# One list of 689 steps replaced by another list of the same steps, in a transformer layer with test-time training

## The chip, the core and the metric

The kernel runs on one core of a Trainium2 chip. Its time is the device time of that core in microseconds, the median of three executions. The profile is one further execution, taken by the hardware profiler.

## The reference

Four sequences of 512 tokens, width 256, all float32. One layer is attention plus feed-forward, each with layer norms and a residual:

```
x = x + layernorm(attn(layernorm(x)))
x = x + layernorm(ffn(layernorm(x)))        # ffn: gelu(x @ proj1.T + b1) @ proj2.T + b2, hidden width 1024
```

`attn` adds two parts and multiplies the sum by `Wo`. One is a sliding-window softmax attention (window 128, two heads of 128). The other carries, for every sequence and each of four heads, three 64x64 weight matrices through the sequence in chunks of 128 tokens. After each chunk its gradient is orthogonalised by five Newton-Schulz passes and the weights are updated:

```
for a, b, c in NS_COEFFS:                   # five times
    A = X @ X.T
    B = b * A + c * (A @ A)
    X = a * X + B @ X
W = renorm(W + X)                           # row norms kept
```

So chunk c+1's small products wait for chunk c's passes; the rest of the layer does not depend on them.

## The kernel before

Everything is cut into 4 chunks of 128 tokens, and each chunk into steps. A step is named by a kind, its chunk and one or two numbers: `NB.2.0.1` is kind NB in chunk 2, pass 0, matrix group 1. One list, `ORDER` (line 137), holds all steps of all chunks. Each engine walks the same list from front to back and issues its own part of every step (the `run(ORDER)` at the end of each engine's block). Parts are tied by semaphores. So the list sets the order on all five queues at once: an engine that waits in one step holds whatever it has behind it. Which PSUM bank a step writes is also worked out from the list (`bank_plan`), the one free longest first, and the step waits for that bank's last reader.

The kinds that matter here, with the line of TensorE's product and the engine that reads it:

- `TX` (L682): transposes X for all heads, four products 128x128; ScalarE copies it to XT (L816).
- `NA` (L691): X times its transpose, 16 products of 64x64 tiles, four at a time in the quarters of the array; VectorE makes A of it (L1056).
- `NB` (L701): A times A, 16 of them; VectorE makes B (L1056).
- `NX` (L713): B times X, 16 of them; ScalarE scales it back into X (L959), in the last pass VectorE adds the weights.
- `RN`, `RM`, `WX` (L723): row norms (a power on GpSimd), scaling on VectorE, transposes of the new weights. Three matrix groups (the last number) go through each of these on their own.
- `FW` (L629), `GB` (L604), `DH` (L617), `OUT` (L643), `DW` (L662): the other small products of a chunk; `MU`, `MR`, `SS` (L673), `SN`: the gradient's norm and X's first value.
- `XT`, `QK` (L559), `VV` (L568), `TR` (L591), `S` (L732), `PT` (L739), `PV` (L748), `CT` (L755), `WO` (L763), `NT` (L770): projections and window attention, with whole 128x128 tiles.
- `F1` (L782): one eighth of the first feed-forward product, GELU on ScalarE (L1034); `F2` (L793): the second, for one sequence; `F2N`: its norm and residual, then a store.

ScalarE keeps one function table at a time and loads another where a step asks for it (L823). A float32 product is issued as two passes of a weight load and a matmul, a transpose as one; one NA, NB or NX is thus 32 loads and 32 matmuls in the trace, a TX four and four, an F1 four and four.

How a small step reads:

```python
def NB(bank, c, it, g):
    take_pair(bank[0], "B", c, 3 * it + g + 1)
    pe.wait_ge(*S["A"](c, 3 * it + g + 1))
    for n in range(4):
        for row, col in QUADS:
            a = A[64 * row:64 * row + 64, g, 4 * (row ^ col) + n, :]
            mm_ = pe.matmul(BANK[bank[0] + row][64 * col:64 * col + 64, n * HD:(n + 1) * HD], a, a, ...)
```

Of the kernel before, what the change touches and what calls it, by code (L numbers as in the profile page):

```python
# [133 lines left out]


ORDER = steps("""
    LN1.0.0 XT.0.0 LNX.0.0 LN1.0.1 LN1.0.2 CO.0 LN1.0.3 LNX.0.1 QK.0.0 XT.0.1 LNX.0.2 LNX.0.3 VV.0.0 VV.0.1 SI.0.0
# [19 lines left out]
    WON.1.1 NA.1.0.0 NA.1.0.1 NA.1.0.2 SI.2.0 SI.2.1 CT.1.2 CT.1.3 L2.1.0 VV.2.2 VV.2.3 NB.1.0.0 NB.1.0.1 NB.1.0.2
    WO.1.2 WO.1.3 NQ.2.0 LN1.3 MS.2 L2N.1.0 NQ.2.1 NX.1.0.0 NX.1.0.1 NX.1.0.2 TX.1.1.0 WON.1.2 WON.1.3 TX.1.1.1
    TX.1.1.2 QK.2.3 NA.1.1.0 NA.1.1.1 NA.1.1.2 NB.1.1.0 NB.1.1.1 SI.2.2 NT.1.0 L2.1.1 L2.1.2 L2.1.3 L2N.1.1 TR.2.0
    TR.2.1 TR.2.2 TR.2.3 MM.2 NB.1.1.2 NX.1.1.0 NX.1.1.1 SM.2 NX.1.1.2 NR.2.0 L2N.1.2 NT.1.1 NT.1.2 L2N.1.3 TX.1.2.0  # L160
    TX.1.2.1 NR.2.1 LNX.3 TX.1.2.2 NT.1.3 NA.1.2.0 F2N.0.0 NA.1.2.1 SI.2.3 NQ.2.2 NQ.2.3 NA.1.2.2 NR.2.2 NR.2.3 KL.2.0
    SP.2 KL.2.1 F1.1.0 F1.1.1 NB.1.2.0 NB.1.2.1 NB.1.2.2 F1.1.2 F1.1.3 NX.1.2.0 NX.1.2.1 NX.1.2.2 TX.1.3.0 F1.1.4
    TX.1.3.1 TX.1.3.2 NA.1.3.0 NA.1.3.1 NA.1.3.2 KL.2.2 F2N.0.1 NB.1.3.0 NB.1.3.1 NB.1.3.2 F1.1.5 NX.1.3.0 NX.1.3.1
    NX.1.3.2 TX.1.4.0 TX.1.4.1 TR.2.4 TX.1.4.2 TR.2.5 TR.2.6 MP.2 KL.2.3 F2N.0.2 NA.1.4.0 NA.1.4.1 NA.1.4.2 TR.2.7
    F1.1.6 NB.1.4.0 F2N.0.3 NB.1.4.1 NB.1.4.2 TR.2.8 F1.1.7 NX.1.4.0 NX.1.4.1 NX.1.4.2 RN.1.0 RN.1.1 RM.1.0 RN.1.2
    TR.2.9 RM.1.1 RM.1.2 F2.1.0 F2.1.1 S.2.0 F2N.1.0 FE.2.0 FE.2.1 WX.2.0 WX.2.1 WX.2.2 F2.1.2 DH.2 FW.2.0 FW.2.1
    F2.1.3 XT.3 GB.2.0 GB.2.1 EL.2.0 EL.2.1 OUT.2.0 OUT.2.1 S.2.1 ELB.2.0 ELB.2.1 OE.2 QK.3.0 QK.3.1 QK.3.2 MU.2.0
    MU.2.1 MU.2.2 DW.2.0 DW.2.1 PT.2.0 PT.2.1 QK.3.3 MR.2.0 MR.2.1 MR.2.2 SS.2.0 S.2.2 SS.2.1 SS.2.2 S.2.3 OY.2 SN.2.0
    PV.2.0 PV.2.1 SN.2.1 SN.2.2 PT.2.2 VV.3.0 PT.2.3 PV.2.2 CT.2.0 F2N.1.1 CT.2.1 TX.2.0.0 TX.2.0.1 TX.2.0.2 NA.2.0.0
    NA.2.0.1 SI.3.0 NA.2.0.2 WO.2.0 WO.2.1 NB.2.0.0 NB.2.0.1 NB.2.0.2 NX.2.0.0 NX.2.0.1 NX.2.0.2 WON.2.0 WON.2.1  # L170
    L2.2.0 TX.2.1.0 TX.2.1.1 TX.2.1.2 PV.2.3 NA.2.1.0 NA.2.1.1 NA.2.1.2 NQ.3.0 F2N.1.2 L2N.2.0 VV.3.1 VV.3.2 NB.2.1.0
# [12 lines left out]
""")


# [1392 lines left out]
```

How the kernel before makes its waits and increments, by code:

```python
        def wait_apart(eng, *waits):  # L409
            waits = [(sem_, n if isinstance(n, int) else eng.to_reg(n)) for sem_, n in filter(None, waits)]
            eng.wait_ge(consts, 1)
            for sem_, n in waits:
                eng.wait_ge(sem_, n)
# [28 lines left out]
        @block.sync  # L443
# [3 lines left out]
            def rows_again(c):  # L447
                for b in range(BATCH):
                    if b or c:
                        sp.wait_ge(*S["x_again"](c, 16 * b))
                    sp.dma_start(x1[:, c % 2, b, :], x[b, bass.ts(c, CHUNK), :]).then_inc(S["x_again"].sem, 16)
# [1 line left out]
            def rows_in(c):  # L453
                sp.wait_ge(*(S["xn"](c - 1, 1) if c > 1 else S["first_xn"](0, BATCH)))
                for b in range(BATCH):
                    if c > 1:
                        sp.wait_ge(*S["x_in"](c, 16 * b))
                    sp.dma_start(x_in[:, b, :], x[b, bass.ts(c, CHUNK), :]).then_inc(S["x_in"].sem, 16)
# [11 lines left out]
            sp.dma_start(b2[:, :], proj2_bias.partition_broadcast(P)).then_inc(ld_misc, 16)  # L471
            sp.dma_start(qk_sc[:, :, :], qk_scale.rearrange("(k p) n -> p k n", p=P)).then_inc(ld_misc, 16)
            sp.dma_start(qk_of[:, :, :], qk_offset.rearrange("(k p) n -> p k n", p=P)).then_inc(ld_misc, 16)
            sp.dma_start(b1[:, :], proj1_bias.rearrange("(k p) -> p k", p=P), allow_slow_non_contiguous=True).then_inc(ld_misc, 16)
            sp.wait_ge(ld_qkv, 16)
            for n, w in enumerate((w1, w2, w0)):
                for i in range(2):
```

## Time and profile before

| | |
|---|---|
| median of 3 runs | 382.11 us |
| lowest, highest | 381.34, 382.75 us |
| span of the profiled execution (from the first to the last instruction) | 380.1 us |
| its own time as a run | not recorded apart from the span |
| TensorE busy | 371.0 us |
| VectorE, ScalarE, GpSimd busy | 257.6, 213.3, 193.9 us |
| DMA | 10.84 MB, 29 GB/s in the mean |

The page splits the span by engine; PE is TensorE's matmuls, PEld its weight loads, DVE VectorE, ACT ScalarE, POOL GpSimd. "The chain that ended last" follows the last instruction back, each time to what released it. "issue" in it is time in which nothing that the profile shows was waited for. Matmuls overlap, so 32 small ones come to far less than 32 times their mean, and a piece of the chain is the better measure of a step.

### The profile page before, as it was taken

How to read it: one execution, taken by the hardware profiler on the slowest of the kernel's cores; microseconds unless marked ns; L12 is line 12 of the kernel's file. 1: busy time of each engine (PE TensorE's matmuls, PEld its weight loads, DVE VectorE, ACT ScalarE, POOL GpSimd, SP SyncE). 2: the span in 40 equal slices, each digit the busy share in tenths (PEclk: the TensorE clock that was granted, in tenths of full speed). 3: DMA queues.
4: the chain of work that ended last, by engine and by line, in shares of the span. 5: the costliest groups of instructions: out<-in, count | busy, mean ns of one | idle time of the engine just before them, and what ended most of it. 6: DMA issues, size and time to landing. Idle time of an engine off the chain costs nothing.

```text
span 380.1 us, 15979 instructions
## 1 busy us (share of the span) xinstructions
PE 371.0 (98%) x6760; PEld 295.4 (78%) x6760; DVE 257.6 (68%) x682; ACT 213.3 (56%) x432; POOL 193.9 (51%) x290
## 2 busy tenths in 40 slices
...
DMA packets 12677, 10.84 MB, mean 29 GB/s; under 512 B 4544, under 2 KB 12096, under 8 KB 12608
## 3 DMA queue, kind: packets, MB, share of 16 engines
...
q8 instruction: 54, 0.88, 1.0%
q14 instruction: 15, 0.12, 0.1%
...
## 4 chain that ended last, share of the span: by engine, by line
PE 86%; DVE 4%; SPq 3%; issue 2%; POOL 2%; ACT 1%; DMA 1%; POOLq 0%; DVEq 0%; ACTq 0%
PE pair L782 15%; PE pair L793 15%; PE pair L713 6%; PE pair L701 6%; PE pair L691 6%; PE pair L559 6%; PE pair L682 5%; PE pair L591 4%; PE pair L763 3%; PE pair L732 3%; PE pair L568 3%; PE pair L748 3%; PE pair L662 2%; PE pair L739 2%; PE pair L629 1%
## 5 line engine op out<-in xcount | busy, mean ns | idle before, releaser
L782 PE MATMUL pair<-xn2T,p1T 128*128 128x512 f32 (+1 forms) x160 | 59.1, 512 | 0.0
L793 PE MATMUL pair<-p2T,h 128*128 128x256 f32 x256 | 57.0, 379 | 0.0
L793 PEld LDWEIGHTS pair<-p2T,h 128*128 128x128 f32 x256 | 48.0, 190 | 6.4 <-issue 0.2
L1424 POOL TENSOR_SCALAR var<-mv 128x1 f32<-128x1 f32 (+1 forms) x55 | 13.1, 239 | 67.1 <-DVE mv L1382 37.4
L1034 ACT ACTIVATE h<-pair,b 128x512 f32<-128x512 f32 (+1 forms) x40 | 23.9, 602 | 36.0 <-PE pair L782 35.9
L782 PEld LDWEIGHTS pair<-xn2T,p1T 128*128 128x128 f32 x160 | 28.7, 190 | 17.1 <-issue 14.8
L1419 POOL TENSOR_TENSOR nq<-ssq,half 128x8 f32<-128x8 f32 (+1 forms) x16 | 24.2, 1513 | 27.5 <-DVE ssq L1141 27.5
L1056 DVE SCALAR_TENSOR_TENSOR A<-pair,eye 128x512 f32<-128x512 f32 x45 | 28.7, 683 | 13.2 <-PE pair L691 13.1
L1419 POOL TENSOR_TENSOR rstd<-var,neg_half 128x1 f32<-128x1 f32 (+1 forms) x55 | 33.5, 609 | 4.6
L1056 DVE SCALAR_TENSOR_TENSOR B<-pair,eye 128x512 f32<-128x512 f32 x45 | 28.9, 684 | 10.2 <-PE pair L701 10.0
L559 PE MATMUL pair<-wqkv,xnT 128*128 128x512 f32 x64 | 31.5, 627 | 0.6 <-ACT xnT L816 0.6
L701 PEld LDWEIGHTS pair<-A 64*64 64x64 f32 x1440 | 23.7, 134 | 7.5 <-issue 4.6
L987 ACT ACTIVATE masked<-masked,nmax 128x256 f32<-128x256 f32 (+1 forms) x32 | 15.1, 474 | 25.5 <-DVE nmax L1298 25.5
L823 ACT ACT_TABLE_LOAD x22 | 28.2, 1283 | 1.1 <-PEq L1569 0.7
L691 PEld LDWEIGHTS pair<-XT 64*64 64x64 f32 x1440 | 23.3, 134 | 6.3 <-issue 5.7
L816 ACT ACTIVATE XT<-pair 128x512 f32<-128x512 f32 x45 | 24.6, 600 | 6.4 <-PE pair L682 6.4
L713 PEld LDWEIGHTS pair<-X,B 64*64 64x64 f32 x1440 | 23.6, 134 | 5.0 <-issue 2.7
L959 ACT ACTIVATE X<-pair 128x512 f32<-128x512 f32 x36 | 19.8, 598 | 13.2 <-PE pair L713 13.1
L701 PE MATMUL pair<-A 64*64 64x64 f32 x1440 | 26.5, 221 | 0.3 <-issue 0.3
L713 PE MATMUL pair<-X,B 64*64 64x64 f32 x1440 | 26.1, 221 | 0.1
L691 PE MATMUL pair<-XT 64*64 64x64 f32 x1440 | 25.8, 221 | 0.3 <-ACT XT L816 0.2
L682 PE MATMUL pair<-ident,X 128*128 128x128 f32 x180 | 24.1, 276 | 0.5 <-ACT X L959 0.3
...
## 6 DMA issues: line engine op xcount, KB each, us to landing
...
```

Of the source, the lines that this page charges most:

```text
L559: mm_ = pe.matmul(ps, xnT[:, k, b * P:(b + 1) * P], wqkv[:, k, 0:512], start=(k == 0), stop=(k == KC - 1))
L682: mm_ = pe.transpose(ps[:, b * P:(b + 1) * P], X[:, g, 2 * b:2 * b + 2, :], ident[:, :])
L691: mm_ = pe.matmul(BANK[bank[0] + row][64 * col:64 * col + 64, n * HD:(n + 1) * HD], xt, xt, start=True, stop=True)
L701: mm_ = pe.matmul(BANK[bank[0] + row][64 * col:64 * col + 64, n * HD:(n + 1) * HD], a, a, start=True, stop=True)
L713: mm_ = pe.matmul(BANK[bank[0] + row][64 * col:64 * col + 64, n * HD:(n + 1) * HD], B[64 * row:64 * row + 64, g, 4 * (row ^ (slot & 1)) + ...
L782: mm_ = pe.matmul(ps[:, at], p1T[:, k, n * P:(n + 1) * P], xn2T[:, k, at], start=(k == 0), stop=(k == KC - 1))
L793: mm_ = pe.matmul(ps[:, 0:DIM], h[:, n, b * P:(b + 1) * P], p2T[:, n, :], start=(n == 0), stop=(n == HC - 1))
L816: return act.activation(dst, src, ACT.Copy)
L823: act.preload_act_table_set(name)
L1034: act.activation(h[:, n, at], BANK[bank[0]][:, at], ACT.Gelu, bias=b1[:, n:n + 1]).then_inc(S["h"].sem, 1)
L1056: return dve.scalar_tensor_tensor(out=out_, in0=in0, scalar=scalar, in1=in1, op0=op0, op1=op1)
L1419: return pool.tensor_tensor(out_, in0, in1, op)
```

## The change

The list `ORDER` is replaced. Both lists hold the same steps, each once. Nothing else in the program is changed; with the list the bank plan changes, and so the banks that a step waits for. Its beginning, before and after:

```diff
 ORDER = steps("""
-    LN1.0.0 XT.0.0 LNX.0.0 LN1.0.1 LN1.0.2 CO.0 LN1.0.3 LNX.0.1 QK.0.0 XT.0.1 LNX.0.2 LNX.0.3 VV.0.0 VV.0.1 SI.0.0
+    LN1.0.0 LNX.0.0 CO.0 XT.0.0 LN1.0.1 LN1.0.2 LN1.0.3 LNX.0.1 QK.0.0 LNX.0.2 VV.0.0 XT.0.1 SI.0.0 XT.0.2 WI.0
...
```

What moves is best seen on TensorE's queue. (In these rows a float32 product counts once, so one NA, NB or NX is x16. The lines of the new file are three higher.) The fourth pass of chunk 0, before: L682 is TX, L782 F1, L691 NA, L543 XT.2, L701 NB, L550 a mean of one step, L713 NX.

```order
L682 MATMUL pair<-ident,X 128x128 x12
L782 MATMUL pair<-xn2T,p1T 128x512 x2
L691 MATMUL pair<-XT 64x64 x48
L543 MATMUL pair<-ident,rows_b 128x128 x8
L782 MATMUL pair<-xn2T,p1T 128x512 x2
L701 MATMUL pair<-A 64x64 x48
L550 MATMUL pair<-ms,ones_avg 64x8 x2
L713 MATMUL pair<-X,B 64x64 x48
```

The same place after; L546 is XT.2, L716 NX, L694 NA, L704 NB, L685 TX, L594 a transpose of TR:

```order
L546 MATMUL pair<-ident,rows_b 128x128 x8
L716 MATMUL pair<-X,B 64x64 x16
L694 MATMUL pair<-XT 64x64 x16
L704 MATMUL pair<-A 64x64 x16
L685 MATMUL pair<-ident,X 128x128 x4
L704 MATMUL pair<-A 64x64 x16
L716 MATMUL pair<-X,B 64x64 x16
L694 MATMUL pair<-XT 64x64 x16
L716 MATMUL pair<-X,B 64x64 x16
L685 MATMUL pair<-ident,X 128x128 x4
L594 MATMUL pair<-ident,silu 128x128 x4
```

Before, each kind runs for all three groups at once with an F1 or an XT in between. After, the groups follow each other a step apart, and two passes overlap.

The first pass of chunk 2, before: L682 is TX, L691 NA, L763 WO, L701 NB, L713 NX.

```order
L682 MATMUL pair<-ident,X 128x128 x12
L691 MATMUL pair<-XT 64x64 x48
L763 MATMUL pair<-wo,aqT 128x256 x4
L701 MATMUL pair<-A 64x64 x48
L713 MATMUL pair<-X,B 64x64 x48
L682 MATMUL pair<-ident,X 128x128 x12
```

And after; L685 is TX, L694 NA, L704 NB, L751 PV, L766 WO, L758 CT, L716 NX:

```order
L685 MATMUL pair<-ident,X 128x128 x8
L694 MATMUL pair<-XT 64x64 x48
L704 MATMUL pair<-A 64x64 x48
L751 MATMUL pair<-v_rows,pT 128x128 x4
L766 MATMUL pair<-wo,aqT 128x256 x2
L758 MATMUL pair<-ident,rows_b 128x128 x2
L716 MATMUL pair<-X,B 64x64 x48
```

Here the WO steps between NA and NB are gone, and PV, a WO and CT stand between NB and NX instead.

## Rows read from the trace of the kernel before

**Rows 1.** the page, engines: busy us (share of the span) and instructions.
```profile
PE 371.0 (98%) x6760; PEld 295.4 (78%) x6760; DVE 257.6 (68%) x682; ACT 213.3 (56%) x432; POOL 193.9 (51%) x290
```

**Rows 2.** the page, shares of the chain that ended last, by engine.
```profile
PE 86%; DVE 4%; SPq 3%; issue 2%; POOL 2%; ACT 1%; DMA 1%; POOLq 0%; DVEq 0%; ACTq 0%
```

**Rows 3.** in order of time: start us, us, engine, instruction, [idle before <-releaser].
```profile
5.28 0.66 PE L536 MATMUL pair<-ident,rows_b 128*128 128x128 f32 x2
...
6.50 3.75 PE L559 MATMUL pair<-wqkv,xnT 128*128 128x512 f32 x4 [0.56 <-ACT xnT L816]
```

**Rows 4.** waits of TensorE: us in total, times, longest us.
```profile
PE pair L732 <- DVE h L1056: 0.4, 1, 0.4
...
PE pair L682 <- ACT X L959: 0.3, 1, 0.3
...
PE pair L591 <- ACT raw L816: 0.3, 1, 0.3
```

**Rows 5.** pieces of the chain that ended last: start us, us, line and instructions.
```profile
40.88 1.72 PE pair L559 x4
...
77.36 1.56 PE pair L691 x96
...
78.92 3.63 PE pair L782 x8
...
100.22 1.46 PE pair L682 x12
...
220.58 1.31 PE pair L723 x12
...
272.10 0.63 PE pair L713 x32
...
289.27 1.09 PE pair L701 x64
...
307.64 6.87 PE pair L782 x16
```

**Rows 6.** the page, the queue of instruction blocks: packets, MB, share of 16 engines.
```profile
q8 instruction: 54, 0.88, 1.0%
```

**Rows 7.** instructions in order of time, 259 to 264 us.
```profile
260.21 1.47 PEld L701 LDWEIGHTS pair<-A 64*64 64x64 f32 x91 [0.33 <-issue]
...
262.07 0.20 PEld L701 LDWEIGHTS pair<-A 64*64 64x64 f32 x5 [0.39 <-issue]
...
262.08 0.33 PE L701 MATMUL pair<-A 64*64 64x64 f32 x5 [0.26 <-issue]
```

**Rows 8.** the same queue of blocks, 259.0 to 260.7 us alone.
```profile
q8 instruction: 1, 0.02, 5.8%
```

**Rows 9.** three stretches: length, busy us (x) of PE, PEld, DVE, ACT, POOL, clock, DMA.
```profile
257.68:262.07 4.39, 4.14 (x139) 3.44 (x131) 3.86 (x9) 1.37 (x2) 2.01 (x5) 1.00 0.12 34
...
262.07:285.71 23.64, 23.63 (x747) 20.68 (x748) 17.39 (x44) 12.33 (x26) 9.57 (x20) 1.00 0.04 10
...
282.09:285.71 3.62, 3.62 (x136) 3.38 (x128) 2.50 (x7) 3.28 (x9) 0.97 (x3) 1.00 0.02 5
```

**Rows 10.** the page, groups of instructions: busy us, mean ns | idle before.
```profile
L1056 DVE SCALAR_TENSOR_TENSOR A<-pair,eye 128x512 f32<-128x512 f32 x45 | 28.7, 683 | 13.2 <-PE pair L691 13.1
...
L823 ACT ACT_TABLE_LOAD x22 | 28.2, 1283 | 1.1 <-PEq L1569 0.7
...
L816 ACT ACTIVATE XT<-pair 128x512 f32<-128x512 f32 x45 | 24.6, 600 | 6.4 <-PE pair L682 6.4
```

**Rows 11.** GpSimd's instructions in order of time, three places.
```profile
44.93 1.15 POOL L1419 TENSOR_TENSOR eye<-ident 128x64 f32<-128x64 f32 x4
...
48.75 1.64 POOL L1419 TENSOR_TENSOR fro<-ss,half 128x8 f32<-128x8 f32 x1 [2.67 <-DVE ss L1240]
...
308.97 4.87 POOL L1419 TENSOR_TENSOR u_n<-u_ss,half 128x8 f32<-128x8 f32 x3 [6.33 <-DVE u_ss L1277]
```

**Rows 12.** instructions in order of time, the last one.
```profile
377.54 0.48 DVE L1056 SCALAR_TENSOR_TENSOR rows_a<-rows_a,rstd,x 128x256 f32<-128x256 f32 x1 [0.29 <-POOL rstd L1419]
```

More of the change, by code:

```diff
@@ L157 @@
[L157 to L171, printed above, removed]
@@ new lines @@
+    TX.0.3.0 F1.0.4 LNX.2 NX.0.2.1 KL.1.1 NQ.1.3 NB.0.2.2 NA.0.3.0 NR.1.2 TX.0.3.1 F1.0.5 NX.0.2.2 NA.0.3.1
+    NB.0.3.0 TX.0.3.2 XT.2 NX.0.3.0 NR.1.3 NA.0.3.2 NB.0.3.1 TX.0.4.0 NB.0.3.2 MP.1 NX.0.3.1 NA.0.4.0 NX.0.3.2
+    TX.0.4.1 TR.1.4 F1.0.6 TR.1.5 TX.0.4.2 NB.0.4.0 NA.0.4.1 KL.1.2 NA.0.4.2 TR.1.6 F1.0.7 S.1.0 NB.0.4.1 KL.1.3
+    NB.0.4.2 NX.0.4.0 RN.0.0 F2.0.0 NX.0.4.1 RN.0.1 RM.0.0 NX.0.4.2 RM.0.1 RN.0.2 F2.0.1 S.1.1 RM.0.2 TR.1.7
+    WX.1.0 TR.1.8 F2.0.2 WX.1.1 WX.1.2 F2N.0.0 TR.1.9 F2.0.3 FE.1.0 LN1.3 FW.1.0 EL.1.0 DH.1 GB.1.0 FW.1.1
@@ new lines @@
+    NQ.2.0 NA.1.1.2 L2.1.1 SI.2.1 NB.1.1.1 NX.1.1.0 NQ.2.1 VV.2.2 CT.1.3 L2.1.2 TX.1.2.0 NB.1.1.2 NR.2.0
+    NX.1.1.1 NA.1.2.0 TR.2.0 F2N.0.2 WO.1.3 TX.1.2.1 NB.1.2.0 NX.1.1.2 VV.2.3 TX.1.2.2 WON.1.3 NA.1.2.1 L2N.1.1
+    NX.1.2.0 NA.1.2.2 NB.1.2.1 TX.1.3.0 TR.2.1 NT.1.1 L2.1.3 NX.1.2.1 L2N.1.2 L2N.1.3 NB.1.2.2 MS.2 MP.2 LNX.3
+    NT.1.2 NR.2.1 TR.2.2 NT.1.3 TX.1.3.1 TR.2.3 MM.2 SI.2.2 SI.2.3 SM.2 NA.1.3.0 NX.1.2.2 NA.1.3.1 F1.1.0 F1.1.1
+    NQ.2.2 NB.1.3.0 NB.1.3.1 NQ.2.3 TX.1.3.2 F1.1.2 NX.1.3.0 NA.1.3.2 NX.1.3.1 F1.1.3 TX.1.4.0 NR.2.2 F1.1.4
@@ new lines @@
+    NR.2.3 NA.1.4.0 NB.1.3.2 TR.2.4 F1.1.5 TX.1.4.1 F2N.0.3 F1.1.6 TR.2.5 NA.1.4.1 NX.1.3.2 NB.1.4.0 TR.2.6
+    TX.1.4.2 F1.1.7 NA.1.4.2 NB.1.4.1 KL.2.0 NX.1.4.0 SP.2 NB.1.4.2 F2.1.0 NX.1.4.1 RN.1.0 RN.1.1 NX.1.4.2
+    RM.1.0 RN.1.2 RM.1.1 TR.2.7 F2.1.1 TR.2.8 RM.1.2 F2.1.2 WX.2.0 KL.2.1 S.2.0 WX.2.1 WX.2.2 F2.1.3 GB.2.0
+    KL.2.2 TR.2.9 KL.2.3 FE.2.0 FW.2.0 FE.2.1 FW.2.1 DH.2 EL.2.0 XT.3 GB.2.1 ELB.2.0 OUT.2.0 EL.2.1 OE.2 OUT.2.1
+    S.2.1 ELB.2.1 QK.3.0 PT.2.0 MU.2.0 QK.3.1 S.2.2 MU.2.1 DW.2.0 MU.2.2 DW.2.1 MR.2.0 PT.2.1 QK.3.2 MR.2.1
```

65 lines of the change are left out of this document (34 added, 31 removed).

## The prediction, made before the changed kernel ran

> **What bounds the kernel now.** I read the page's first table, then the chain of waits, then the stretches of the chain in order of time. TensorE is busy 371.0 of 380.1 us [rows 1] and the chain of the work that ended last lies on it for 86% [rows 2]. So every term below is time on TensorE's queue; VectorE, ScalarE and GpSimd (68, 56 and 51% busy) count only where TensorE waits for them.
>
> TensorE's first transposing step begins at 5.28 us, the last step of the list (F2.3.3) at 371.34. These 366.1 us I split in four. I gave each of its 461 steps the least time that its kind took in this trace between such neighbours; they add up to 354.6 us, the work. The start loses 3.5 us: QK.0.0 takes 3.75 us [rows 3] where four such products take 1.72 later [rows 5], its input comes late, and TR.0.0 waits 0.3 us for a copy [rows 4]. About 0.7 us are stops in the middle of steps, which no semaphore explains (next part). The rest, 7.3 us, is spread over some fifty waits for other engines, the largest of 0.3 to 0.5 us [rows 4].
>
> **Part 1: the work, which no wait hides.** All steps stay, but TensorE pays for changing between small products (64x64, 64x128) and whole ones. Three small steps between whole ones take 1.56 us, two 1.09 [rows 5]; so one more costs 0.47, and a run of small steps costs 0.15 beyond that. On the other side two F1 steps between small runs take 3.63 us, half of the unbroken four's 6.87 is 3.44: 0.19 more. Twelve transposing products between small runs take 1.46, twelve elsewhere 1.31: 0.15 more [rows 5]. One change in and out costs 0.30 to 0.35 us. Counting the list, the small steps stand in 54 runs before and in 65 after: 11 x 0.30 to 0.35 is 3.3 to 3.9 us. The same least times laid on the new neighbours give 358.3, that is +3.7, which I take. Bounds: +3.3 and +4.0. Nothing covers it: it is TensorE's own time.
>
> **Part 2: instruction blocks.** TensorE's 6,760 loads and 6,760 matmuls [rows 1] and some 410 waits come in over a queue of 54 packets of 16 KB [rows 6], about 256 records each. Does that ever stop TensorE? In the three steps NB.2.0.0 to NB.2.0.2, 91 of 96 loads run, then, in the middle of the last step and with no semaphore to wait for, TensorE stands for 0.4 us "for nothing", then come the last five [rows 7]. One block was on the way until shortly before (one packet in 1.7 us, 5.8% of 16 engines' time, or 1.6 us; the mean packet takes 1.0% x 380.1 x 16 / 54 = 1.1 us) [rows 6, 8]. Lesser stops inside steps lie at 59.97, 257.68 and 285.71 us. From 257.68 to 262.07 there are 131 loads and 139 matmul records (with those still running at the edge), from 262.07 to 285.71 748 loads [rows 9]: one block, and six. In my count of the queue the four places have the same remainder by 256 to within 6 records. So TensorE does run dry at block borders, and while it works through one block the next is still on its way.
>
> How long must a block last? One with a slow packet was held to 4.39 us; the quickest stretch of 256 records took 3.62, with a stop of 0.1 [rows 9]. With packets of 1.1 us instead of 1.6 the first would be 3.9. I take 3.5 as the need, 3.0 and 3.9 as its bounds. Now I lay the same borders on both lists, a small step being 65 records, four transposing products 9, an F1 8. Before: the shortest block is 3.43 us of work, the next 3.63, 3.66, 3.77. After: 1.94 (NA.2.0.2 to NB.2.0.2, nothing between them), 2.49 (NB.0.3.1 to NX.0.3.2), then 3.33, 3.36, 3.39, 3.39, 3.44, 3.60. The first has some 0.45 us of data waits inside. Shortfalls against 3.5: 1.1 + 1.0 + 0.6 for the five = 2.7 us, 0.7 before: +2.0. With a need of 3.0 it is +0.4; with 3.9 about +4.
>
> The Trainium skill speaks against this term: "Runtime: NRT & Kernel Launch", section "Instruction fetch mechanics", says that the sequencer fetches 16 KiB blocks on its own queue and that crossing a border is mostly hidden. By that rule this part would be nought. The trace agrees on the size of the block (16 KB) and not on the hiding at 262.07 us; that case is a rival below.
>
> **Part 3: waits for other engines.** Here the new list gains. Where it leaves one of the four round trips of a pass (TX to NA over ScalarE, NA to NB and NB to NX over VectorE, NX to TX over ScalarE), I took TensorE's work between the two steps. A copy on ScalarE takes 0.60, an A or B on VectorE 0.68 us [rows 10]; the shortest round trips took 0.93 to 1.04. Before, 12 trips by way of VectorE have only two small steps (0.93 us) between, and three over ScalarE 0.58 to 0.83; after, it is 9 and none. The three big single losses of before go: NB x3 with NX x3 right behind, TX.2.3.2 close behind its NX, S.1.1 behind its bank [rows 4, 7].
>
> The longer chains I followed. SS.0.2 to TX.0.0.2: GpSimd's power 1.7, its addition 0.3, the new place of EY 1.15 ahead of it, VectorE 0.9, together 5.2 us with hand-overs, and 5.5 us of TensorE's work stand between (7.0 before). NX.2.4.2 to WX.3.2: three powers of 1.6 in a row [rows 11]; work between falls from 8.2 to 6.6 us, but the first of the three now starts an F1 earlier, and I find W ready at 6.3. DW.1.1 asks for its last input at 11.0 us after FW.1.0 and gets it at 11.05. All hold, by 0.1 to 0.3 us: no cover is left, and whatever is later than I think shows. ScalarE has 24 table loads for 22 (1.28 us each [rows 10]); the new pair in the third pass of chunk 0 holds it for 3.0 us, while TensorE has 7 us until TX.0.3.0: nothing.
>
> What can't go: the A and B rows come every 0.68 us [rows 10] where TensorE takes 0.47 to 0.52, so triples cost some 0.4 each time (1.2 in all), PV.3.2 to CT.3.2 has 1.08 us for a trip of 1.66 (0.5), and small ones of 0.08 (0.9). That is 2.6. For what I overlook I add 0.9: 3.5 us, so -3.8. Bounds: 2.0 (-5.3) and 6.0 (-1.3).
>
> **Part 4: the ends.** VV.0.1 now has a transpose (0.22 us) between it and XT.0.1, on whose copy it waits, where a VV (0.93) stood: +0.3 (0 to 0.5). At the end F2N.3.2 moves ahead of F2.3.3, but the end hangs on F2.3.3's power [rows 12]: nothing. Some of the stops of part 2 fall where TensorE would wait for data anyway: -0.7.
>
> **Sum.** 3.7 + 2.0 - 3.8 + 0.3 - 0.7 = +1.5 us. The profiled execution has a span of 380.1 us, 2.0 less than the median of the runs; I leave that distance as it is: 382.1 + 1.5 = 383.6 us.
>
> **Rivals.**
> - *Slower: the fetch sets the pace of the dense stretches.* Need 3.9 us, as the one clean stop says after its slow packet is taken off. Then the dozen shortest blocks, all under 3.9 us, are held, +4.0 in part 2; with 4.0 us of waits and 0.9 of overlap: 3.7 + 4.0 - 3.3 + 0.3 - 0.9 = +3.8, 385.9 us. It leaves "no change" from a need of about 3.6. For it: 4.39 us at 262.07. Against: the one stretch of 3.62.
> - *Faster: the list does away with the waits.* Waits 2.0, no stop at a border: 3.7 - 0.7 - 5.3 + 0.3 = -2.0, 380.1 us. For it: every chain that I followed just holds. Against: 3.7 us of changes must be earned first, and 7.3 is all there is.
> - *The blocks don't matter.* The stops of before are something else, or need stays under 3.0: 3.7 - 0.7 - 3.8 + 0.3 = -0.5, 381.6 us. That is the time by the skill's rule, too. Against: four stops at one remainder.
>
> **How the numbers follow.** A measurement of this kernel tells about 0.5% (1.9 us) from no change. The forecast and the last rival, both within that, have 0.42 together (0.28 and 0.14). Slower has 0.38: the first rival 0.25, the rest the upper side of the forecast's own spread. Faster has 0.20, the second rival. The forecast's own range is 381.5 to 385.5. The bounds added up reach 380.4 and 388; for 8 in 10 I take 380.0 to 387.2.
>
> **What would show it.** Part 1: in the chain, single small steps of 0.62 us and transposing fours of 0.59 in place of triples. Part 2: loads of L704 and L716 with a stop "issue" in the middle, in the first pass of chunk 2 and the fourth of chunk 0, and 256 records never under 3 us; with two clean passes there, part 2 is wrong. Part 3: no wait of TensorE over 0.3 us after 25 us; if the ones of TX and S remain, the gain isn't there. The forecast is wrong if the span falls under 378 or goes over 385.

## The result, and the profile after

The changed kernel takes 396.05 us (median of 4 runs, 394.09 to 396.38) against 381.86 us of before (4 runs, 381.34 to 382.75): ratio 1.036, 95% interval 1.0333 to 1.0387. That is 14.2 us more, where 1.5 us more was forecast and 387.2 us was the upper end of the range. The profiled execution has a span of 394.4 us and took 396.4 us.

The page of after: engines, the queue of instruction blocks, and the chain by engine [rows 1, 6, 2 of before]:

```profile
PE 378.3 (96%) x6760; PEld 297.4 (75%) x6760; DVE 262.9 (67%) x682; ACT 220.2 (56%) x434; POOL 198.0 (50%) x290
...
q8 instruction: 54, 0.88, 0.9%
...
PE 28%; POOL 3%; DVE 2%; issue 1%; POOLq 0%; DVEq 0%
```

TensorE is busy for 7.3 us more and idle for 7.0 us more. The chain explains only a third of the span here: it broke off on the way back, so I read its steps from the instructions in order of time instead. The waits of TensorE in after [rows 4]: us in total, times, longest.

```profile
PE pair L539 <- DVE rows_b L1090: 2.5, 2, 2.3
PE pair L704 <- issue: 1.5, 2, 0.8
PE pair L773 <- DVE rows_b L1350: 1.1, 3, 0.5
...
PE pair L716 <- issue: 0.9, 1, 0.9
PE pair L685 <- DVE X L1255: 0.8, 2, 0.5
PE pair L665 <- issue: 0.8, 1, 0.8
PE pair L751 <- ACT pT L819: 0.6, 1, 0.6
```

Two kinds of wait have come: "issue" in the middle of small steps (L704 is NB, L716 NX), and waits for results of other engines (L539 XT in the start, L773 NT, L685 TX, L751 PV). L665 belongs to the second kind, though the profile says "issue": it is DW.0.0, which by the program waits for GpSimd's KL steps, and it starts when the last of them has ended:

```profile
43.11 0.61 POOL L1422 TENSOR_TENSOR vl<-silu,lr 128x256 f32<-128x256 f32 x1
...
43.82 0.69 PE L665 MATMUL pair<-A,vl 128*64 128x64 f32 x16 [0.82 <-issue]
```

In before the same product of GpSimd ended at 36.6 us, since the four KL steps stood together, ahead of WX.0.0; the new list spreads them from S.0.0 to ELB.0.0.

For every run I made the same account. From the start of XT.0.0 to the start of F2.3.3, each step gets the least time of its kind between such neighbours ("work"; the rule and the table of least times are those of the prediction, so this row is worked out from the list and not measured; what is left after it is measured). What a step takes beyond that is put under "borders" if a border of 256 records falls into it, under "waits" if not and if it is over 0.06 us, else under "rest".

| us | before | after | b_ph60 | b_ph120 | a_ph60 | a_ph204 | b_split | h_c0 | a_sum |
|---|---|---|---|---|---|---|---|---|---|
| in all | 366.1 | 380.4 | 370.8 | 375.2 | 381.3 | 375.7 | 372.1 | 376.5 | 373.9 |
| work | 354.6 | 358.3 | 354.6 | 354.6 | 358.3 | 358.3 | 358.1 | 357.1 | 357.1 |
| borders | 1.4 | 5.8 | 6.8 | 11.3 | 7.2 | 1.5 | 1.4 | 4.8 | 3.3 |
| waits | 8.7 | 15.0 | 8.2 | 7.9 | 14.6 | 14.2 | 11.2 | 13.2 | 12.2 |
| rest | 1.4 | 1.3 | 1.3 | 1.4 | 1.2 | 1.7 | 1.4 | 1.4 | 1.3 |

Before to after: work +3.7, borders +4.4, waits +6.3, rest -0.1, together 14.3 us. The waits grew everywhere: 4.1 to 5.7 us up to 30 us, 0.8 to 2.6 from there to 62, 0.6 to 1.2 to 128, 0.7 to 1.5 in 150 to 232, 1.2 to 2.1 in 250 to 330, 0.4 to 1.0 behind. The largest: 2.45 us at XT.0.3, 0.8 at DW.0.0, 0.74 at PV.1.1, 0.74 at NT.3.1, 0.63 at TX.2.0.2, 0.61 at TX.0.0.0.

The largest one, in order of time (start us, us, engine, instruction, [idle before <-releaser]):

```profile
13.54 0.63 DVE L1358 COPY W<-X 128x128 f32<-128x128 f32 x4 [2.11 <-DMA X<-in_L_attn_w_dram]
14.09 0.76 DVE L1362 COPY W<-X 128x512 f32<-128x512 f32 x2
14.77 0.41 DVE L1090 TENSOR_SCALAR rows_b<-x_in,mv,rstd 128x256 f32<-128x256 f32 x1
...
15.23 0.44 PE L539 MATMUL pair<-ident,rows_b 128*128 128x128 f32 x2 [2.28 <-DVE rows_b L1090]
```

VectorE stands at WI.0 for its transfer; LNX.0.3, which XT.0.3 needs, is queued behind it. And the windows of after behind that stop (length, busy us of PE, PEld, DVE, ACT, POOL, clock, DMA):

```profile
15.00:16.00 1.00, 0.77 (x4) 0.70 (x5) 0.59 (x3) 1.00 (x4) 0.00 (x0) 0.92 0.00 0
16.00:17.00 1.00, 1.00 (x3) 0.68 (x2) 0.54 (x1) 0.92 (x3) 0.00 (x0) 0.50 0.63 172
...
19.00:20.00 1.00, 1.00 (x3) 0.40 (x3) 1.00 (x4) 0.00 (x0) 0.70 (x2) 0.87 0.00 0
```

After 2.3 us without a product the granted clock is 0.50, the lower level of 1.2 GHz, for some 3.5 us, and VV.0.2 and QK.0.2 pay 1.7 us for that. At the border of 106.1 us in after [rows 7 and 9 of before], first TensorE's products, then the stretch from the border before:

```profile
104.01 0.65 PE L694 MATMUL pair<-XT 64*64 64x64 f32 x32
104.63 0.56 PE L716 MATMUL pair<-X,B 64*64 64x64 f32 x21
106.12 0.45 PE L716 MATMUL pair<-X,B 64*64 64x64 f32 x11 [0.93 <-issue]
```

```profile
102.18:106.12 3.94, 3.02 (x128) 2.56 (x126) 2.40 (x4) 1.19 (x2) 3.94 (x6) 1.00 0.12 37
```

21 of 32 products of NX.0.3.2 run, then nothing for 0.93 us and no semaphore to wait for: the 256 records since 102.18 held only 3.0 us of work. Such stops in after stand at 106.1, 171.9, 185.0, 189.7, 273.6 and 316.4 us, 0.4 to 1.2 us each.

### The profile page after: what moved, and what is told of

Same layout as the page of the kernel before. It is cut to its first block and busy times, and to the rows that moved or that the text cites. A ratio compares the mean times of both kernels' runs of the same rounds, so it can differ in the third digit from the quotient of the medians.

```text
span 394.4 us, 15983 instructions
## 1 busy us (share of the span) xinstructions
PE 378.3 (96%) x6760; PEld 297.4 (75%) x6760; DVE 262.9 (67%) x682; ACT 220.2 (56%) x434; POOL 198.0 (50%) x290
## 5 line engine op out<-in xcount | busy, mean ns | idle before, releaser
L1059 DVE SCALAR_TENSOR_TENSOR A<-pair,eye 128x512 f32<-128x512 f32 x45 | 30.4, 685 | 14.9 <-PE pair L694 14.8
L819 ACT ACTIVATE XT<-pair 128x512 f32<-128x512 f32 x45 | 26.8, 595 | 16.6 <-PE pair L685 16.2
L704 PEld LDWEIGHTS pair<-A 64*64 64x64 f32 x1440 | 25.6, 134 | 8.9 <-issue 8.2
L704 PE MATMUL pair<-A 64*64 64x64 f32 x1440 | 30.5, 222 | 1.5 <-issue 1.5
L716 PEld LDWEIGHTS pair<-X,B 64*64 64x64 f32 x1440 | 25.5, 134 | 7.8 <-issue 7.1
L716 PE MATMUL pair<-X,B 64*64 64x64 f32 x1440 | 30.3, 221 | 1.2 <-issue 0.9
L694 PE MATMUL pair<-XT 64*64 64x64 f32 x1440 | 29.5, 220 | 0.3 <-issue 0.3
L685 PE MATMUL pair<-ident,X 128*128 128x128 f32 x180 | 27.8, 278 | 1.0 <-DVE X L1255 0.8
L694 PEld LDWEIGHTS pair<-XT 64*64 64x64 f32 x1440 | 25.3, 135 | 3.8 <-issue 3.6
L685 PEld LDWEIGHTS pair<-ident,X 128*128 128x128 f32 x180 | 20.5, 141 | 6.2 <-issue 4.0
```

Source lines behind the costliest of these rows:

```text
L685: mm_ = pe.transpose(ps[:, b * P:(b + 1) * P], X[:, g, 2 * b:2 * b + 2, :], ident[:, :])
L819: return act.activation(dst, src, ACT.Copy)
L1059: return dve.scalar_tensor_tensor(out=out_, in0=in0, scalar=scalar, in1=in1, op0=op0, op1=op1)
```

## The experiments

Medians, before on the same chip, and the ratio with its 95% interval. The four runs of after lie between 394.09 and 396.38 us, so a median within about 1 us of 396.05 (a_dense, a_waits, h_start, a_chain, a_oy, a_all_oy) is not told from after. Names with b_ start from the list of before, those with a_ or h_ from that of after (396.05 us, 1.036).

| run | us | before | ratio |
|---|---|---|---|
| b_ph60 | 387.59 | 381.91 | 1.0146 (1.0124 to 1.0169) |
| b_ph120 | 391.11 | 381.70 | 1.0240 (1.0224 to 1.0255) |
| a_ph60 | 398.95 | 381.70 | 1.0445 (1.0419 to 1.0471) |
| a_ph204 | 393.70 | 381.91 | 1.0312 (1.0275 to 1.0349) |
| b_split | 388.13 | 381.97 | 1.0158 (1.0140 to 1.0176) |
| a_dense | 395.44 | 381.97 | 1.0346 (1.0319 to 1.0373) |
| a_wi | 394.39 | 381.70 | 1.0321 (1.0300 to 1.0342) |
| b_wi | 385.85 | 381.70 | 1.0104 (1.0083 to 1.0125) |
| a_waits | 395.45 | 381.97 | 1.0352 (1.0331 to 1.0373) |
| h_start | 395.73 | 382.01 | 1.0350 (1.0323 to 1.0378) |
| a_chain | 395.66 | 382.01 | 1.0342 (1.0316 to 1.0368) |
| a_all | 394.01 | 382.01 | 1.0310 (1.0283 to 1.0336) |
| a_oy | 396.38 | 381.91 | 1.0380 (1.0357 to 1.0403) |
| a_all_oy | 395.30 | 381.91 | 1.0344 (1.0322 to 1.0366) |
| h_c0 | 392.65 | 381.97 | 1.0275 (1.0245 to 1.0305) |
| a_sum | 391.10 | 381.97 | 1.0241 (1.0213 to 1.0270) |
| b_warm | 381.96 | 381.97 | 0.9996 (0.9987 to 1.0006) |
| b_best | 381.77 | 382.01 | 0.9994 (0.9983 to 1.0005) |

### The borders of the instruction blocks, moved under an unchanged list

```diff
+            for n in range(39):      # b_ph120; b_ph60 and a_ph60: 15, and the nine below stay; a_ph204: 55, and five stay
+                pe.matmul(BANK[7][0:8, 0:8], ones[:, 0:8], ones[:, 0:8], start=True, stop=True)
-            for n in range(9):
-                pe.matmul(BANK[7][:, (n % 4) * P:(n % 4 + 1) * P], ones[:, :], ones[:, :], start=True, stop=True)
```

> The list of before, unchanged; only the nine large warm-up products at the start (36 records of TensorE) are replaced by 39 of 8x8 (156 records), so that every border between instruction blocks of 256 records falls 120 records earlier in the list. Theory fetch: a border costs nothing or something by how much work lies between it and the one before; by the step times, blocks of before shorter than 3.5 us miss 0.06 us in sum where the borders lie now and 11 us with this shift (5.7 us with 3.0 us per block): from TR.0.0 to the end the time grows by 6 to 12 us, all of it at positions 183 records before a multiple of 256. Rival (the blocks don't matter; the stops of before were waits for something else): the stretch from TR.0.0 to the end stays within 0.7 us of before's. The start itself may move by up to 2 us by the other warm-up.

> The list of before with 15 products of 8x8 (60 records) ahead of the warm-up: borders 60 records earlier, half the shift of b_ph120. Theory fetch, by amount: blocks under 3.5 us miss 7.5 us in sum here (11.3 for the shift of 120, where 9.4 us were measured; 0.06 without a shift), and a block behind a stopped border needs about 1 us more than one behind a clean border, which makes 9: from TR.0.0 to the end 5.5 to 9 us more than before. Rival (a shift as such costs, whatever the list): the same 9.4 us as with 120, or nothing.

> The list of after, unchanged; 15 products of 8x8 (60 records) are added ahead of the warm-up, so the borders fall 60 records earlier in the list. Theory fetch: the sum of what blocks are shorter than 3.5 us grows from 3.2 to 7.5 us (for 3.0 us: from 1.6 to 3.6), so from TR.0.0 to the end it takes 2 to 4.5 us more than after. The stops at 106.1, 172, 189.7, 273.6 and 316.4 us go and others come 60 records away from a multiple. Rival (blocks don't matter): the stops stay where they are in the list, and only the start is 0.5 to 1.5 us later.

> The list of after with its borders 204 records earlier, which is 52 later (55 products of 8x8 and five large ones for warm-up). By the same rule (3.45 us for a block behind a clean border, 4.45 behind a stopped one) the missing time is 4.4 us where it is 7.2 without a shift: the stops at borders make 3 to 4.5 us where they made 5.8, so from TR.0.0 to the end 1 to 3 us less than after; the start takes up to 2 us more for the other warm-up. Rival: the stops have their places in the list and stay at 5.8 us.

The direction is that of the fetch in all four, and the amount in b_ph120 and b_ph60. In the traces a_ph60 stayed under what was expected (1.2 us from TR.0.0 on, not 2 to 4.5) and a_ph204 gave back more (4.7 us, not 1 to 3). Both were profiled in the fastest of their four runs and after in its slowest: the medians differ from after by +2.9 and -2.4 us, with a warm-up that ends 0.6 and 0.9 us later. From TR.0.0 to F2.3.3 the list of before takes 351.1 us, with its borders 60 records earlier 356.7, 120 earlier 360.4; that of after 363.2, 60 earlier 364.4, 204 earlier 358.5. The place shows the cause: counted along the list, the large stops in the middle of steps are at remainder 192 by 256 in after, at 72 in b_ph120 (nine of nine) and at 132 in b_ph60 and a_ph60 (all of 6 and of 7). So a shift of 120 moved them by 120, and one of 60 by 60. The waits outside the borders did not change (8.7, 8.2, 7.9 us). TensorE's waits in b_ph120, then the worst stop there:

```profile
PE pair L713 <- issue: 3.2, 4, 1.0
...
PE pair L691 <- issue: 2.2, 3, 1.3
PE pair L682 <- issue: 1.1, 1, 1.1
```

```profile
293.15 0.68 PE L691 MATMUL pair<-XT 64*64 64x64 f32 x29
295.11 0.33 PE L691 MATMUL pair<-XT 64*64 64x64 f32 x3 [1.28 <-issue]
295.37 0.66 PE L682 MATMUL pair<-ident,X 128*128 128x128 f32 x4
```

Before had 0.3 us of such waits at L701 in its whole trace. That a shift as such costs nothing is shown by a_ph204, which is faster than after although its warm-up ends 0.9 us later.

Taken over the traces of 17 of the kernels here: TensorE resumes 1.42 us after the packet of the block has landed (64 stops, eight in ten of them 1.26 to 1.53). The packet starts 0.9 us after the border before when that one was crossed without a stop (median of 455), but 2.2 us after it when TensorE had been stopped there (median of 75). With 1.0 us for the packet, I estimate from these medians that a block needs 3.3 us in the first case and 4.6 in the second, so a stop makes the next one likelier. The single cases scatter around that: behind an unstopped border eight packets in ten start 0.5 to 2.6 us after it. So there is no sharp limit. Over all 20 traces TensorE went through 43 blocks in under 3.3 us, and at the end of 36 it then stood for 0.2 us or more. At the other seven it hardly did or not at all; one is in b_ph120, where the packet had started 0.66 us ahead of the border:

```profile
198.53:200.68 2.15, 2.15 (x139) 2.14 (x135) 1.62 (x3) 0.67 (x2) 0.00 (x0) 1.00 0.00 0
```

### Work in place of a stop

```diff
- TX.0.3.2 XT.2 NX.0.3.0 NR.1.3 NA.0.3.2 NB.0.3.1 TX.0.4.0 ... TR.1.4 F1.0.6 TR.1.5
+ TX.0.3.2 XT.2 NX.0.3.0 NR.1.3 NA.0.3.2 NB.0.3.1 F1.0.6 TX.0.4.0 ... TR.1.4 TR.1.5
- NA.2.0.2 NB.2.0.0 WON.2.0 NB.2.0.1 L2.2.0 NB.2.0.2 PV.2.3 WO.2.1
+ NA.2.0.2 PV.2.3 WO.2.1 NB.2.0.0 WON.2.0 NB.2.0.1 L2.2.0 NB.2.0.2
```

> The list of after with three whole-size steps moved into two stretches that were nearly all small steps: F1.0.6 behind NB.0.3.1, and PV.2.3 and WO.2.1 behind NA.2.0.2. The work stays the same (one run more, 0.36 us), but the instruction blocks that end at 106.1 and 273.6 us last 1.7 us longer by work. Theory fetch: the stops of 1.20 and 1.02 us at these two borders go, a part of up to 0.8 us comes back at the border behind the first one, since F1.0.6 is missing there: 0.7 to 1.9 us less than after, 394.2 to 395.4. Rival (the stops belong to the steps, NX.0.3.2 and NB.2.0.2, or to what these wait for): the stops stay at these two steps, and the time grows by the 0.4 us of the added run.

The stops at both borders are gone (1.20 and 1.02 us in after), so they belong to the blocks and not to these steps. But one block later, where F1.0.6 is now missing, the first is back:

```profile
109.68 1.10 PE L694 MATMUL pair<-XT 64*64 64x64 f32 x61
111.58 0.33 PE L694 MATMUL pair<-XT 64*64 64x64 f32 x3 [0.81 <-issue]
```

1.12 us at NA.0.4.2. In place of the second, 0.4 and 0.70 us appear at NB.2.0.2 and NX.2.0.2, as waits for VectorE. Net 0.6 us in the median, a little under the low end of what was expected and not told from nothing.

### The price of one more run of small steps

```diff
- F1.0.1 ... F1.0.2 ... NB.0.2.0 NB.0.2.1 NB.0.2.2      (and nine places like it)
+ F1.0.1 ... NB.0.2.0 F1.0.2 NB.0.2.1 NB.0.2.2
```

> The list of before with ten whole-size steps moved one small step inward (F1.0.2 behind NB.0.2.0, F1.0.4 behind NX.0.2.0, and so on), so that ten runs of small steps are cut in two: 64 runs instead of 54, nothing else changes. Theory switch (each run of small steps costs 0.30 to 0.35 us beside the work in it): from TR.0.0 to the end 3.0 to 3.5 us more than before, spread over the ten places as about 0.33 us each, with up to 1 us of new waits on top: 384.7 to 386.2 us. Rival (a change of tile shape costs no time of its own; what after lost comes from the fetch and from waits alone): within 0.7 us of before.

Seven of the ten places cost 0.353 to 0.357 us each, one (TR.1.8, four transposing products) 0.307; at NX.0.1.1 (0.395) and NX.1.2.1 (0.875) a wait stands on top. In a place such as F1.0.2 all four steps around the two new changes are longer: by 0.09 and 0.10 us the F1, by 0.11 and 0.05 the NB. Work by the rule grows by 3.5 us. So the price is shown, with 0.355 us a run. The total came out 6.0, not 3.0 to 4.5, and the trace has the rest in one line: WO.1.3, moved by one small step, now takes another bank, and NA.1.1.1 waits for the step that frees it.

```profile
170.81 0.69 PE L694 MATMUL pair<-XT 64*64 64x64 f32 x32
173.51 0.70 PE L694 MATMUL pair<-XT 64*64 64x64 f32 x33 [2.00 <-DVE wo_n L1338]
```

### The start

```diff
- SI.0.0 XT.0.2 WI.0 LNX.0.3 VV.0.1 NQ.0.0 QK.0.1 SI.0.1 XT.0.3          (a_wi; b_wi does the reverse:
+ SI.0.0 XT.0.2 LNX.0.3 VV.0.1 NQ.0.0 QK.0.1 SI.0.1 XT.0.3 WI.0           WI.0 ahead of LNX.0.3)
+ LN1.0.0 XT.0.0 LNX.0.0 ... WX.0.2 S.0.0 S.0.1                (h_start: before up to S.0.1,
  DH.0 WN.0 VV.1.0 VV.1.1 FW.0.0 GB.0.0 ...                     then what is left in the order of after)
```

> The list of after with one step moved: WI.0 (VectorE copies the tables W from the staged transfer, which lands at 13.5 us) comes after XT.0.3 and no longer stands ahead of LNX.0.3. Theory start: WI.0's wait for its transfer holds VectorE from 11.4 to 13.5 us, so LNX.0.3, XT.0.3 and all of TensorE behind it stand for 2.4 us, and TensorE then goes at the granted clock of 0.76 on average until 20 us; without it TR.0.0 starts at 18.3 to 19.5 us instead of 22.5, and the whole is 3.0 to 4.2 us shorter than after, 391.8 to 393.1. Rival: the transfers of the start set the pace (WX.0.0 needs the same tables) and the stop only moves behind TR.0.0: under 1 us shorter, 395 or more.

> The list of before with that one step moved the other way: WI.0 ahead of LNX.0.3. Theory start: XT.0.3 can't start before about 15.2 us where it started at 12.6, so the time grows by 2.5 to 4 us, half of it the wait and half a lower granted clock behind it: 384.4 to 386. Rival: nothing in the start matters so long as the transfers land when they do: within 0.7 us of before.

> The list of before up to S.0.1 (26.9 us in its trace), then what is left in the order of after. Theory start: up to 30 us the list of after loses 2.2 us more than that of before, and not by WI.0 alone (putting WI.0 back moved TR.0.0 2 us forward, and S.0.1 only 0.3 us): the order of all engines' steps up to S.0.1 is what costs it, so S.0.1 starts 1.8 to 2.6 us earlier than in after (after correction for DH.0, which comes behind it here) and the whole is 1.5 to 2.6 us shorter: 393.4 to 394.6. Rival: what follows S.0.1 is held by other engines and gives it back: under 0.7 us less than after.

In b_wi the theory holds: XT.0.3 waits 3.47 us, the products behind it go at the lower level, TR.0.0 starts 4.1 us later, and the time is 4.15 us more. In a_wi it falls for size, and the time of 394.39 us lies between what theory and rival gave. TR.0.0 starts 1.9 us earlier (20.57), but TensorE then waits for VectorE's tttT (DH.0, 0.43 us; S.0.1, 0.44) and S.0.1 starts only 0.3 us earlier. Of the 1.9 us that its profiled execution is shorter, 1.1 come from smaller stops at borders (5.8 to 4.7 us), which differ by that much between executions. h_start brings TR.0.0 forward by 2.1 us and VV.1.0 by 1.7, of which 0.65 are left at CT.0.0; its time is 0.3 us below after, as the rival said. The stop at WI.0 is an error of the new list, but the next engine in line was late by nearly as much.

### The waits for other engines, step by step

```diff
- PV.0.1 SN.0.1 TX.0.0.0 WO.0.0 PV.0.2          SS.1.1 PV.1.1 PT.1.2 SN.1.0 SS.1.2 VV.2.0     (a_waits)
+ PV.0.1 SN.0.1 WO.0.0 PV.0.2 TX.0.0.0          SS.1.1 VV.2.0 PV.1.1 PT.1.2 SN.1.0 SS.1.2
- PV.2.2 TX.2.0.1 TX.2.0.2                      NT.3.0 NT.3.1 WO.3.3
+ TX.2.0.1 PV.2.2 TX.2.0.2                      NT.3.0 WO.3.3 NT.3.1
```

> The list of after with four steps moved over a neighbour: TX.0.0.0 behind PV.0.2, PV.2.2 behind TX.2.0.1, VV.2.0 behind SS.1.1, WO.3.3 behind NT.3.0. The number of runs of small steps and the borders of the instruction blocks stay. Theory data: the four waits of 0.61, 0.63, 0.74 and 0.74 us there are for results of other engines that come too late for this order, and a step put in front hides them: 2.0 to 2.6 us less than after, 393.4 to 394.0. Rival: what TensorE waits for is itself late because TensorE came late (a chain through all engines), and the wait comes back one step on: under 1 us less.

The rival's time and its sign hold: under 1 us, and the four waits came back one step on, nearly to the hundredth: 0.61 as 0.14 at WO.0.0 and 0.48 at TX.0.0.1; 0.74 as 0.84 at TX.1.0.0; 0.63 as 0.17 and 0.43; 0.74 as 0.73 at F1.3.0.0. That they are late because TensorE came late is not shown by this; a result that is late by another engine's own queue would look the same.

```diff
- S.0.3 SS.0.2 PV.0.1 ... VV.1.3        MR.1.1 S.1.2 PT.1.1        (a_chain; and from PV.3.2 on the order of before)
+ S.0.3 SS.0.2 VV.1.3 PV.0.1 ...        MR.1.1 PT.1.1 S.1.2      (a_all: all of this behind the start of h_start)
```

> The list of after with the waits for other engines treated at the other engines' end: VV.1.3 behind SS.0.2 (more work of TensorE while GpSimd makes fro: 2.55, 1.66 and 1.65 us in a row), S.1.2 behind PT.1.1 (ScalarE copies pT before it loads a table and masks), and the last part, from PV.3.2 on, in the order of before. Theory chain: the four waits moved over a neighbour in the run before came back one step on (0.61 as 0.14 and 0.48, 0.74 as 0.84, 0.63 as 0.17 and 0.43, 0.74 as 0.73), so another engine's queue sets them; here those at TX.0.0.0, PV.1.1 and NT.3.1 go, 1.5 to 2.4 us less than after; at the borders near 60 us up to 0.7 us may come on top, since VV.1.3 is missing there. Rival: TensorE's own order sets them, as in the run before: within 0.7 us of after.

> The start of h_start and the three changes of a_chain together. If start and waits are separate causes, the gains add up: 3 to 5 us less than after, 391 to 393, and what is left against before is eleven more runs of small steps at 0.31 us (3.4 us) and the stops at the borders (4 to 5 us): 389.5 to 392. Rival: the waits of one place are the slack of the next, and together they give no more than the larger of the two.

a_chain is 0.4 us below after, within the rival's 0.7. Only the part in which every engine's order is that of before lost its wait for good: behind 330 us the waits fell from 1.0 to 0.1. PV.1.1 gained 0.73 and TX.1.0.0 gave 0.57 of it back. With VV.1.3 ahead the 0.61 us at TX.0.0.0 went, and 0.94 came at NX.0.0.0, where VV.1.3 had stood and covered a wait for VectorE's B: 0.3 us more in all. a_all is 2.0 us below after by the medians; 3 to 5 were expected.

### GpSimd held by VectorE

```diff
- SS.0.0 OY.0 PV.0.0 ... S.0.3        SS.1.0 OY.1, S.1.3 ahead        SS.2.0 OY.2, S.2.3 ahead
+ SS.0.0 S.0.3 OY.0 PV.0.0 ...        SS.1.0 S.1.3 OY.1               SS.2.0 S.2.3 OY.2
```

> The list of after with S.c.3 moved between SS.c.0 and OY.c in chunks 0, 1 and 2, so that VectorE, after it has copied ss for GpSimd, masks scores (0.9 us) before it makes the product y*out_f (OY, 1.21 us). Theory lock: in after GpSimd's fro starts 0.16 us after this product and is held by it, 2.55 us in place of 1.64 in before; with another operation first, the first fro of each chunk takes 1.65 us again, and the waits behind it (0.61 at TX.0.0.0, 0.63 at TX.2.0.2) shrink: 0.6 to 1.8 us less than after. Rival: the 2.55 us are the price of the first power after another function on GpSimd, whatever VectorE does: fro stays 2.55, the waits stay, within 0.5 us of after.

> The list of a_all (start of before, three changes to the order of the other engines, end of before) with the three moves of a_oy. Theory lock: a further 0.6 to 1.5 us less than a_all: 392.4 to 393.4. Rival: a_all within 0.5 us, since in the first chunk the waits there have moved on already.

After, then a_oy, in order of time [rows 11 have this fro in before, 1.64 us]:

```profile
51.05 1.21 DVE L1227 TENSOR_TENSOR y<-y,out_f 128x1024 f32<-128x1024 f32 x1
51.21 2.55 POOL L1422 TENSOR_TENSOR fro<-ss,half 128x8 f32<-128x8 f32 x1 [2.68 <-DVE ss L1243]
```

```profile
51.52 1.64 POOL L1422 TENSOR_TENSOR fro<-ss,half 128x8 f32<-128x8 f32 x1 [2.67 <-DVE ss L1243]
...
52.01 1.22 DVE L1227 TENSOR_TENSOR y<-y,out_f 128x1024 f32<-128x1024 f32 x1
```

The lock is shown: 2.55, 2.54, 2.55 us in the three chunks of after and in a_all, 1.64 in all six of a_oy and a_all_oy. With the product started first GpSimd is held for 0.9 us; with fro started first nobody loses. The Trainium skill, "SBUF — State Buffer", section "Who interferes with whom", has that rule (VectorE with two inputs in SBUF and a reading GpSimd share one pair of ports, and who issues first keeps it). The trace agrees where VectorE issues first (2.55 us for 1.64). Where GpSimd does, it doesn't: VectorE's product takes 1.22 us inside fro's 1.64, as long as ever, and here the measurement decides. The time does not follow: a_oy is no faster than after (396.38), since S.c.3 covered a wait where it had stood: TX.0.0.0 waits 0.44 us less, but CT.0.0 and SS.0.2 together 0.63 more; PV.1.1 waits 0.74 less, but SS.1.0 0.82 more. The 1.3 us by which a_all_oy lies over a_all are borders (5.0 to 6.4 us) and waits.

### Whole stretches from before

```diff
-    LN1.0.0 LNX.0.0 CO.0 XT.0.0 ... CT.0.0 ... WO.0.0 ... TX.0.0.2      (after)
+    LN1.0.0 XT.0.0 LNX.0.0 LN1.0.1 ... TX.0.0.0 TX.0.0.1 CT.0.1 NA.0.0.0 NA.0.0.1 SI.1.2 CT.0.2 WO.0.1 TX.0.0.2      (h_c0: before)
     NB.0.0.0 ...      (from here on what is left, in the order of after; a_sum: from PV.3.2 on in that of before)
+            for n in range(61):      # a_sum alone, ahead of five large ones in place of nine
+                pe.matmul(BANK[7][0:8, 0:8], ones[:, 0:8], ones[:, 0:8], start=True, stop=True)
```

> The list of before up to TX.0.0.2 (57 us in its trace), then what is left in the order of after; 61 runs of small steps where after has 65. Theory stretch: the waits of the start (1.6 us more than before) and of the first chunk up to 62 us (1.8 more) belong to the order of all engines' steps over that stretch, and with it and four runs less (1.2 us) the time is 3.5 to 4.8 us less than after: 391.3 to 392.6. Rival: the rest of the list, made for the other beginning, gives most of it back, as it gave back two thirds of the start's 1.7 us: 0.5 to 2 us less than after.

> h_c0 with the end of before from PV.3.2 on and the borders 228 records earlier (61 products of 8x8 and five large ones for the warm-up). By what the runs so far gave: h_c0's gain, 0.9 us for the end, and 2 to 4 us for the borders, less 1 us for the longer warm-up: 386.5 to 390 us; left against before are seven runs of small steps (2.2 us) and 2 to 3 us of waits in the second and third chunk. If it stays over 391, the causes do not add up.

h_c0 is 3.4 us under after by the medians (3.5 to 4.8 were expected), 3.9 in the account: work 1.2, waits 1.8, borders 1.0. The borders were not meant: behind the stretch they lie where they did, and stops there differ by that much between executions. Of the 3.4 us of waits that the stretch has more in after, 1.8 stay away; behind the seam new ones come, 0.90 us at NX.0.0.0 and 0.72 at NB.0.0.2, both for VectorE. So a stretch taken over with all its engines' orders keeps about half its gain in waits here, and all of it at the end of the list, where nothing follows (1.0 us from h_c0 to a_sum). a_sum, at 391.1, stays over the 386.5 to 390 expected, and over the 391 from which on, by what was set down before, the causes do not add up as I had counted them: the borders gave 1.5 us and not 2 to 4. Against before it still has 2.5 us of work, 1.9 at borders, 3.5 of waits and a warm-up 1.2 us longer, which is its 9.1 us.

### Two tries to beat before

```diff
+                    if b == 0:                                                                  # b_warm, behind XT.0.0
+                        pe.matmul(BANK[7][:, 0:P], ones[:, :], ones[:, :], start=True, stop=True)
```

```diff
- S.1.1 S.1.2 PT.1.0 QK.2.0     TX.2.3.2 NT.2.2     CT.2.1 TX.2.0.0 TX.2.0.1     CT.3.1 PV.3.3      (b_best)
+ QK.2.0 S.1.1 S.1.2 PT.1.0     NT.2.2 TX.2.3.2     TX.2.0.0 TX.2.0.1 CT.2.1     PV.3.3 CT.3.1
```

> The list of before with one more 128x128 warm-up product right behind XT.0.0, where TensorE has been standing for 0.56 us. In some profiled executions the three passes of QK.0.0 behind that stop come every 854 ns, in others every 429. Theory: the stop is what makes them slow, and filling it gives 1.0 to 1.8 us (380 to 380.7). Rival: the slow passes have to do with something else (the load just before, the transfer under way), and the time is that of before within 0.4 us.

> The list of before with four steps moved over a neighbour at its own waits: QK.2.0 behind FW.1.1 (0.51 us waited at S.1.1), NT.2.2 behind NA.2.3.1 (0.43 at TX.2.3.2), CT.2.1 behind TX.2.0.1 (0.34 at TX.2.0.2), CT.3.1 behind PV.3.3 (0.22 at CT.3.1). If TensorE's own order sets these waits: 0.8 to 1.4 us less than before, 380.6 to 381.2. If another engine's queue does, as in after, they come back one step on: within 0.4 us of before.

Neither moves the time (12 runs each). None of the versions is faster than before.

## Why the prediction was wrong, step by step

**What bounds it.** Right: all of it is time on TensorE's queue, and the split into work, stops and waits held with other sizes. The three terms added to +1.9 us and were +14.4.

**Part 1, work, +3.7.** Right. The +3.7 of the account is the prediction's own number, laid on again; what measures it is b_split, with 0.355 us for a run on its own. For eleven that is 3.9 us, between the forecast's +3.7 and its upper bound of +4.0; the 0.30 to 0.35 read from the chain were a little low.

**Part 2, blocks, +2.0 (0.4 to 4).** The mechanism was right and the place of the stops too (NX.0.3.2 and NB.2.0.2 are the two shortest blocks that it named), the size was not: +4.4. The mis-sized term is the need of a block, taken as one number of 3.5 us. In the median it is 3.3 us behind a clean border and 4.6 behind a stop, and it scatters with the start of the packet, so blocks with over 3.5 us of work were held too, as those that end at 171.9 and 189.7 us (4.4 and 4.7 us with their stops of 0.5 and 1.0). For the first of them the packet started 2.0 us after a clean border. The sum also had a slip: it took off the 0.7 us of stops measured in before, where its own rule gives before 0.07 (one block of 3.43 us); like for like it is +2.6. The rule of the Trainium skill that a crossing is mostly hidden ("Runtime: NRT & Kernel Launch", "Instruction fetch mechanics") fits the list of before, which loses 1.4 us at some 50 borders, and not dense stretches: 11.3 us with the same list in b_ph120.

**Part 3, waits, -3.8 (-5.3 to -1.3).** This is the step that failed: the waits were to shrink by 3.8 us and grew by 6.3 with the start, 4.7 without. It counted, trip by trip, whether TensorE's work between two steps covers the shortest round trip, and credited each trip that did. That takes the other engines as free when TensorE hands over. They are not: they run through the same list in order, 50 to 67% busy, and a result queues behind whatever the list puts in front of it. Three cases show it: LNX.0.3 behind WI.0 (b_wi: one step moved on VectorE, 4.15 us), KL.0.3's product 7 us later on GpSimd (0.8 us at DW.0.0; gone in h_start, where 0.64 us at PT.0.0 came instead), and the fro behind OY. I followed SS.0.2 to TX.0.0.2 and not SS.0.0 to TX.0.0.0, which has the 0.61 us, 0.44 of them gone in a_oy. Of the three chains "that just hold", WX.3.2 held; TX.0.0.2 waits 0.22 us and DW.1.1 0.26. "No cover is left, and whatever is later than I think shows" was the right sentence, and the term should have followed it instead of taking the gain.

**Part 4, the ends, +0.3 and nothing.** The start cost 1.6 us: WI.0's place ahead of LNX.0.3 was in the shown diff, and I read the diff for TensorE alone. The end was not nothing: 0.6 us more, most of it at NT.3.1 (0.74). The overlap of stops and waits (-0.7) can't be told from the account.

**The rivals.** The "slower" one had the right side for one of the right reasons (+4.0 at the borders; its need of 3.9 us for every block is not what the packets show) and still ended at 385.9, since it took over -3.3 from part 3. "The blocks don't matter" is refuted by b_ph60 and b_ph120. All of them shared part 3's sign; a rival in which the waits grow was missing.

**Open.** What each of the added waits hangs on is not settled. Shown is that they are not TensorE's order alone, not GpSimd's fro alone, not the start alone, and that at the end of the list they went with all engines' orders those of before, in the first chunk by half. For the second and third chunk (1.7 us more) that wasn't tried.
